# A four-layer transformer on one core: row weights loaded during the last attention, output done tile by tile, last handover re-ordered

## The reference

```
out = layer_norm(x + sigmoid(x @ gate_w + gate_b) * broadcast) * gamma + beta
```

## Time and profile before

| what | value |
|---|---|
| median of 3 runs | 4440.16 us (4436.63 to 4440.83) |
| profiled execution, its own time | 4444.07 us |
| its span, first to last instruction | 4442.3 us |
| mean granted PE clock | 0.928 of full speed |
| busy: PE, DVE, ACT, POOL | 85%, 55%, 36%, 33% |
| DMA moved | 585.42 MB, mean 132 GB/s |

### The profile page before, as it was taken

One profiled execution on the slowest core, in us unless ns is written; L12 is line 12 of the kernel. 1 busy time (PEld: TensorE's weight loads), 2 busy tenths in 40 slices (PEclk: granted clock), 3 DMA queues, 4 the chain that ended last, 5 costly groups with the idle time before them and its releaser, 6 DMA issues.

```text
span 4442.3 us, 53426 instructions
## 1 busy us (share of the span) xinstructions
PE 3769.3 (85%) x19032; PEld 2729.7 (61%) x19032; DVE 2423.0 (55%) x4270; ACT 1582.0 (36%) x2683; POOL 1447.2 (33%) x1732
## 2 busy tenths in 40 slices
PE   6877999999999999999999999999999998774300
PEld 4755776677657776777667766776577756442100
DVE  5643565366545664556546653665456644542477
ACT  4422434433443435343534344334434352220000
POOL 2421541244124521353124412441245213020266
PEclk9989999999999999999999999999999999766655
DMA  6464532444325332443235324443253323013222
GB/s 234 154 236 188 186 137 89 157 142 139 128 86 199 128 143 77 174 160 137 86 144 176 140 88 157 143 139 128 86 199 129 133 77 119 15 58 116 71 95 80
DMA packets 176147, 585.42 MB, mean 132 GB/s; under 512 B 14752, under 2 KB 15008, under 8 KB 171280
## 3 DMA queue, kind: packets, MB, share of 16 engines
q1 hardware_dynamic: 167056, 565.24, 35.7%
q10 hardware_dynamic: 8832, 16.78, 1.0%
HBM read 494.39 MB, written 87.05 MB: 131 GB/s over the span
## 4 chain that ended last, share of the span: by engine, by line
PE 65%; DVE 14%; POOL 7%; ACT 6%; issue 5%; DMA 3%; SPq 0%; DVEq 0%; POOLq 0%; ACTq 0%
PE ps_P L1577 24%; PE ps_Y L1577 10%; PE ps_E L1577 5%; PE ps_O L1577 4%; PE ps_O L1768 4%; PE ps_E L1750 3%; PE ps_T L1577 3%; PE ps_T L1729 3%; POOL pT_lo L721 3%; DVE pf L1164 2%; PE ps_T L1733 2%; POOL rstd L829 2%; ACT probs L957 1%; ACT pT_hi L844 1%; DVE stats L1070 1%
## 5 line engine op out<-in xcount | busy, mean ns | idle before, releaser
L1577 PE MATMUL ps_P<-XnT_hi,w_ring 128*128 128x512 f32 x3328 | 1079.5, 406 | 66.1 <-DVE XnT_lo L1046 14.5
L1577 PEld LDWEIGHTS ps_P<-XnT_hi,w_ring 128*128 128x128 f32 x3328 | 608.5, 191 | 230.4 <-issue 72.2
L1577 PE MATMUL ps_P<-XnT_lo,w_ring 128*128 128x512 f32 x1664 | 659.3, 396 | 0.0
L1270 DVE TENSOR_REDUCE row_max<-ps_T 128x1 fp32r<-128x384 f32 (+3 forms) x768 | 425.6, 595 | 277.1 <-PE ps_T L1733 277.0
L957 ACT ACTIVATE probs<-ps_E 128x512 f32<-128x512 f32 (+2 forms) x768 | 362.2, 524 | 451.1 <-PE ps_E L1750 303.5
L721 POOL TENSOR_TENSOR pT_lo<-pf,pT_hi 128x512 fp32r<-128x512 f32 x320 | 410.6, 1291 | 301.0 <-ACT pT_hi L844 296.0
L739 POOL TENSOR_SCALAR_AFFINE_SELECT probs<-probs 128x512 f32<-128x512 f32 x256 | 162.5, 635 | 1037.8 <-ACT probs L957 1037.8
L786 POOL TENSOR_TENSOR hT_lo<-hf,hT_hi 128x512 fp32r<-128x512 f32 x128 | 164.8, 1287 | 638.5 <-ACT hT_hi L844 638.5
L1577 PEld LDWEIGHTS ps_P<-XnT_lo,w_ring 128*128 128x128 f32 x1664 | 317.5, 191 | 70.5
L1577 PE MATMUL ps_Y<-w_big,hT_hi 128*128 128x512 f32 x896 | 333.8, 419 | 24.9 <-DVE y_acc L1294 12.6
L712 POOL TENSOR_TENSOR sines<-swapped,sinT 128x512 f32<-128x512 f32 x160 | 213.8, 1336 | 377.8 <-ACT swapped L844 371.7
(11 more groups left out here) (259 smaller groups left out, 7135.5 us busy)
## 6 DMA issues: line engine op xcount, KB each, us to landing
w_ring<-split_dram SPq DMA_DIRECT2D x412, 512.0 KB, 3.4
w_big<-split_dram SPq DMA_DIRECT2D x63, 2048.0 KB, 7.7
dec<-decay SPq DMA_DIRECT2D x32, 1024.0 KB, 4.8
split_dram<-w_ring SPq DMA_DIRECT2D x58, 512.0 KB, 4.2
split_dram<-w_big SPq DMA_DIRECT2D x36, 512.0 KB, 4.4
wo1w<-split_dram SPq DMA_DIRECT2D x8, 2048.0 KB, 7.8
gatew<-split_dram SPq DMA_DIRECT2D x8, 2048.0 KB, 10.2
X<-x SPq DMA_DIRECT2D x8, 1024.0 KB, 10.5
```

The costliest lines, as they stand in the source:

```text
L1270: dve.reduce_max(row_max[:, g % 2, i_, m0:m0 + len(heads)], ps[TB[half]][:, 0:len(heads) * w].rearrange("p (n s) -> p n s", s=w), AX_X)\
L1577: last = pe.matmul(dst, stat[s_], mov[m_], start=first_ and k == 0, stop=last_ and k == n - 1)
```

## The change

1. Memory: `d1w` and `d2w` get the place of `w_big`, `XnT` and `w_ring`, which are dead in the last attention; `aggw`, `bcw`, `thought`, `rows`, `bias1` lie over the feed-forward's buffers; the seven constants, gamma and beta lie in `X` and `y_acc`.
2. Row weights: in round 8 SP issues 16 transfers right after the handover's stores (`row_weights`), and nine of 1 MB in slots 8, 11, ..., 32 (`row_feed`). Block 7's x3 and gate are no longer stored; its last row is copied from `xr` into `rows`.
3. Handover of round 8: SP issues the ring units first. Block 6's front goes to `XnT` and its gate weights to `w_big`; its four gate products are made in slots 1, 2, 6 and 8 (banks E0, E1), the bias additions a slot later, the sigmoids at slot 10. DVE and POOL do block 7's layer-2 statistics, norms and residuals tile by tile, mixed with block 6's front.
4. After the slots: block 7's four gate products stand behind the first four phases of the row chain, its sigmoids behind the tenth. The chain uses one PSUM bank (P1) for all.
5. Broadcast: instead of a store and eight loads, eight matmuls of a column of the identity with `rows`, into all eight PSUM banks.
6. Output: tile by tile. The first norm isn't made as such: mean times rstd of all 32 tiles (`pd_shift`) is made once on POOL from moments kept from the gate's front; ACT scales x3 by its rstd (`fin_first`, the first of the two activations below), DVE subtracts the shift and adds the gated row. The last norm is ACT's scaling (`fin_last`) and a DVE instruction that subtracts the shift and adds x3. DVE works on tiles k, k-1 and k-3 in one iteration. POOL has only 128x1 operations. Loads go through a ring of three blocks, SP issues loads and stores, and block 7 is taken from `xr` and `y1`.

```diff
+FIN_RING, FIN_SKEW = 3, 3
+LAST_GATE_AT = (1, 2, 6, 8)
+SIGMOID_AT = 9
+FEED_AT = {8 + 3 * m: m for m in range(9)}
# SP, round 8
-                    x2_store(c)
                     for k in range(UNITS_A, UNITS_A + UNITS_C):
                         unit(n, k)
+                    gate_weights(c - 1)
+                    x2_store(c)
+                    row_weights(c)
...
+                        if n == NB and s in FEED_AT:
+                            row_feed(FEED_AT[s])
+                        if s == SLOTS - 1 and c == NB - 1:
+                            sp.dma_start(rows[c:c + 1, :], xr[P - 1:P, NT - 1, :]).then_inc(last_row_in, 16)
...
# POOL, output
+            for k in range(NF + 1):
+                if k < NF:
+                    fin_rstds(k, 0, eps_ffn)
+                if k:
+                    n = 4 + (k - 1) % 4
+                    fin_rstds(k - 1, 1, eps)
+                    pool.wait_ge(*fin_rstd[1].need(k - 1))
+                    pool.tensor_tensor(var_eps[:, n:n + 1], moments[:, n, 0:1], rstd[:, n:n + 1], ALU.mult).then_inc(*fin_shift2.hit(k - 1))
# ACT, output
+                act.activation(fin_h[:, k % 4, :], fin_place(k)[0], ACT.Copy, scale=pd_rstd[:, k:k + 1]).then_inc(*fin_h_done.hit(k))
...
+                act.activation(z, z, ACT.Copy, scale=rstd[:, n:n + 1]).then_inc(*fin_w.hit(k))
...
+            for k in range(NF + 1):
+                if k + 3 < NF:
+                    fin_first(k + 3)
+                if k:
+                    fin_last(k - 1)
# DVE, output
+            for k in range(NF + FIN_SKEW):
+                new, mid, old = k, k - 1, k - FIN_SKEW
+                    dve.tensor_tensor(z, ps[BC_BANKS[b]][:, :], z, ALU.mult)
...
+                    dve.scalar_tensor_tensor(z, z, rstd[:, n:n + 1], bet, ALU.mult, ALU.add)
...
+                    dve.scalar_tensor_tensor(z, fin_h[:, new % 4, :], pd_shift[:, new:new + 1], z, ALU.subtract, ALU.add)
...
+                    dve.scalar_tensor_tensor(z, z, var_eps[:, n:n + 1], x3_, ALU.subtract, ALU.add)
...
+                    fin_measure(new, 0, fin_sum.need(new))
+                    fin_measure(mid, 1, fin_affine.need(mid))
+                    fin_aggregate(new, 0)
+                    fin_aggregate(mid, 1)
+                    dve.scalar_tensor_tensor(z, z, moments[:, n, 0:1], gam, ALU.subtract, ALU.mult)
...
# PE
+                    if n == NB and s in LAST_GATE_AT:
+                        t = LAST_GATE_AT.index(s)
+                        gate_product(d, t, EB[t % 2], XnT, WB)
...
-            for t in range(NT):
-                gate_product(NB - 1, t)
+            for m, phase in enumerate(PHASES):
+                row_phase(*phase)
+                if m < NT:
+                    gate_product(NB - 1, m, FB[m], YnT, gatew)
+            for b in range(NB):
+                pe.matmul(ps[BC_BANKS[b]][:, :], ident[0:R, b:b + 1].to_broadcast([R, P]), rows[:, :], start=True, stop=True)
```

More of the change, by code:

```diff
@@ L64 @@
 WO_AT = {2: 2, 5: 3}
+PHASES = [("pre", 0, "T"), ("pre", 0, "agg")]
+PHASES += [("step", g, k) for g in range(K_STEPS) for k in ("T", "d1", "tr", "d2", "sum")]
+PHASES += [("post", 0, "T"), ("post", 0, "bc")]
+FIN_RING, FIN_SKEW = 3, 3
 SLOTS = 12 * NQ
@@ new lines, in build @@
+        ROW_INS = 16 * 25
+        NF = NB * NT
+        fin_in = [count(f"fin_in{n}", NB // FIN_RING + 1, step=32) for n in range(FIN_RING)]
+        fin_sent = [count(f"fin_sent{n}", NB // FIN_RING + 1, NT, step=16) for n in range(FIN_RING + 1)]
+        fin_bc, fin_shift = count("fin_bc", NB), sem("s_fin_shift")
+        fin_h_done, fin_w = count("fin_h", NF), count("fin_w", NF)
+        fin_gated, fin_sum, fin_scaled, fin_affine, fin_out = (count("fin_" + k, NF) for k in ("gated", "sum", "scaled", "affine", "out"))
@@ new lines, in build, with fin_place, moments_of @@
+        fin_stats, fin_moments = ([count(f"fin_{k}{n}", NF) for n in range(2)] for k in ("stats", "moments"))
+        fin_rstd, fin_shift2 = [count(f"fin_rstd{n}", NF) for n in range(2)], count("fin_shift2", NF)
+        BC_BANKS = ("P0", "P1", "T0", "T1", "E0", "E1", "O", "Y0")
+        def fin_place(k):
+            b, t = divmod(k, NT)
+            return (xr[:, t, :], y1[:, t, :]) if b == NB - 1 else (fin_x[:, b % FIN_RING, t, :], fin_z[:, b % FIN_RING, t, :])
+        def moments_of(kind, b, t):
+            n = KINDS.index(kind) * NT + t
+            return pd_moments[:, b * NT + t, :] if kind == "pd" else moments[:, n, :]
@@ L478, in build, with rstd_of @@
+        def rstd_of(kind, b, t):
+            n = KINDS.index(kind) * NT + t
+            return pd_rstd[:, b * NT + t:b * NT + t + 1] if kind == "pd" else rstd[:, n:n + 1]
         block = ctx.enter_context(nc.Block())
@@ new lines, in _ @@
+            for b in range(FIN_RING):
+                fin_load(b)
+            for k in range(NF):
+                b, t = divmod(k, NT)
+                slot = b % FIN_RING if b < NB - 1 else FIN_RING
+                sp.wait_ge(*fin_out.need(k))
+                sp.dma_start(out[b, t * P:(t + 1) * P, :], fin_place(k)[1]).then_inc(*fin_sent[slot].hit(b // FIN_RING if slot < FIN_RING else 0, t))
+                if t == NT - 1 and b + FIN_RING < NB - 1:
+                    sp.wait_ge(*fin_sent[slot].need(b // FIN_RING, NT - 1))
+                    fin_load(b + FIN_RING)
@@ L685, in _ @@
+            for slot in range(FIN_RING):
+                sp.wait_ge(*fin_sent[slot].need((NB - 2 - slot) // FIN_RING, NT - 1))
+            sp.wait_ge(*fin_sent[FIN_RING].need(0, NT - 1))
         @block.gpsimd
@@ L752, in _ @@
                     rope(n, 0)
-                if c >= 0:
+                if c >= 0 and n < NB:
                     for t in range(NT):
@@ L757, in _ @@
                         residual("qb", resid_b, c, t, X[c % 2][:, t, :], y_acc[:, t, :])
+                elif c >= 0:
+                    for t in range(NT + 3):
+                        if t < NT:
+                            rstds("qb", c, t)
+                        if t >= 1 and t <= NT:
+                            residual("qb", resid_b, c, t - 1, X[c % 2][:, t - 1, :], y_acc[:, t - 1, :])
+                        if t >= 3:
+                            rstds("pc", c, t - 3)
+                    pool.wait_ge(*down.need(c, NQ - 1, NT - 1))
+                    pool.memset(rows[:, :], 0.0).then_inc(s_rows_clear, 1)
                 if n < NB:
@@ new lines, in row_phase, with fin_rstds @@
+            def row_phase(stage, g, what):
+                if stage == "pre" and what == "T":
+                    row_rstds("pre", 0, 0, eps)
+                    row_rstds("pre", 0, 1, eps_ffn)
+                elif stage == "step" and what == "T":
+                    row_rstds("step", g, 0, eps_ffn)
+            for phase in PHASES:
+                row_phase(*phase)
+            def fin_rstds(k, m, eps_):
+                n = m * 4 + k % 4
+                pool.wait_ge(*fin_moments[m].need(k))
+                pool.tensor_tensor(var_eps[:, n:n + 1], moments[:, n, 1:2], eps_[:, :], ALU.add).then_inc(*ln_var.hit())
+                pool.wait_ge(*ln_var.need())
+                pool.tensor_tensor(rstd[:, n:n + 1], var_eps[:, n:n + 1], minus_half[:, :], ALU.pow).then_inc(*fin_rstd[m].hit(k))
@@ new lines, in _ @@
+            for m, phase in enumerate(PHASES):
+                row_phase(*phase)
+                if m < NT:
+                    gate_product(NB - 1, m, FB[m], YnT, gatew)
+            pe.wait_ge(*row_at(row, "post", 0, 2))
+            for b in range(NB):
+                if BC_BANKS[b] in empties:
+                    pe.wait_ge(*empties[BC_BANKS[b]])
+                pe.matmul(ps[BC_BANKS[b]][:, :], ident[0:R, b:b + 1].to_broadcast([R, P]), rows[:, :], start=True, stop=True)\
+                    .then_inc(*fin_bc.hit(b))
```

488 lines of the change are left out of this document (256 added, 232 removed).

## The result

The kernel after takes **4261.87 us** (median of 4 runs, 4257.73 to 4273.22) against 4440.49 us for the kernel before beside it: ratio 0.9607, 95% interval 0.9595 to 0.9618. The forecast was 4286 us with a range from 4268: the direction was right and the gain too small, 154 us forecast and 179 us measured, 6 us outside the range.

A forecast was written before the change was run, and what follows sets the result against it. TensorE is full up to 3737 us; a 705 us tail with little overlap follows, its output (266.6 us) longest. Terms -5.5-48.1+12.0-8.4-104.1 = -154.1 us, put on the median 4440.16, gave 4286 us, range 4268 to 4316.

The forecast's parts named there:

- Handover: Last down product to block 7's first query/key/value product: weights issued first and gate products gone, -14 us.
- Block 6's gates: Four gate products moved into attention slots: +3 us in slots 1 and 2, +5 in 6 and 8, bias additions +0.5.
- Late attention: Last attention, to the end of the residual: 25 added transfers on queue SP cost 0 us.
- Start of the row chain: Residual to first row statistic: weights already there, the chain waits only for DVE's last subtraction, -48.1 us.
- Block 7's gates: Four gate products between the row steps, partly in PE's waits: +12.0 us, bounds 7.2 and 18.5.
- Broadcast: Row's round trip through memory replaced by a K=32 matmul into PSUM: -8.4 us, bounds -8.6 and -7.9.
- Output: Final output stage: 4.85 us a tile plus 7.3 us end, 162.5 against 266.6 us, -104.1 us.
- Rival 1: Output: rstd late because POOL waits out DVE instructions, every tile stalls 0.75 us, +24 us, 4310 us; chance 0.12.
- Rivals 2 to 4: Attention held up, 4310 us, chance 0.08; weights not early, 4317 us, 0.03; POOL starved in the output, 4451 us, 0.01.

The follow-up runs named there:

- three variants that read 49 us: Kernel after with nine row-weight loads behind the last attention slot (4283.05 us), one more POOL addition per output tile (4272.29 us), or output not interleaved (4305.87 us).
- again: Kernel after, unchanged, run for more executions and a second profile: 4262.14 us, ratio 0.9605.
- the kernel with the cut: Kernel after with block 7's four gate products in the row chain cut from 12 matmuls to 1 each: 4260.59 us, ratio 0.9597.

## Why the prediction was wrong, point by point

In the first profile the tail got 33.5 us shorter than the sum had it: 10.3 in the row chain with block 7's gates, 7.4 where block 6's gates went, 6.9 in the output, 5.6 in the attention and 3.3 in the handover.

- **Handover, -14 forecast, -17.3 measured: right in mechanism.** The working gave 15.5 and took 1.5 off for POOL stretching VectorE's norms. Two norms were stretched and VectorE's work came out 0.9 us longer than worked out, but the product followed the front by 1.7 us less.
- **Block 6's gates, +8 forecast with +0.5 for DVE, +1.1 measured.** Priced by themselves they cost 5.3 to 6.6 us, so the term was 1.4 to 2.7 us too high, 1.3 of it in slots 6 and 8, where I took the higher price for a clock of 0.68; in this profile the slots ran at 1.00 (3787.5 to 3806.5). The larger part is what I had no term for: the matmuls around them ran faster. The kernel before with constants in its attention shows it without any gate: 40.7 us at a clock of 0.92, where it took 43.0 at 0.74. In the three variants that read 49 us the same slots ran at 0.78, and there the term would have been +6.0.
- **Late attention, 0 forecast, -5.6 measured.** Mostly the same cause: with the constants both kernels take 160 to 161 us at 0.98 and 0.99 (163 us at 0.96 in the two kernels that fill the row chain too).
- **Start of the row chain, -48.1 forecast, -48.2 measured: right**, and for the stated reason (VectorE's last subtraction ends it).
- **Block 7's gates, +12.0 forecast, +1.7 (again: +5.0) measured: the step that failed most.** Their own price was near: some 9 us for eleven twelfths of them against the kernel with the cut, or 10 to 11 us if the shortening of the nine weight products (8.2 us; again 43.6 instead of 49.7, 6.1) is added to what the stage grew by. The step that failed is that I priced an added product only by its own duration and left the products behind it at the durations of the kernel before, which had been measured behind idle stretches. Against the kernel with the cut, the gate products gave back 4.8 us (again: 2.7) in these nine; the other 3.4 us have no cause shown.
- **Broadcast, -8.4 forecast, -8.3 measured: right.**
- **Output, -104.1 forecast, -111.0 measured.** The sum of start-to-start times, 4.66 us, was right to 0.01. The failing term is the 0.2 us a tile that I put on top for the tight rstd (5.8 us), and the end, 6.2 us instead of 7.3. Rival 1 had the right weak place. It stayed away by next to nothing: with the extra POOL operation, rstd was 0.26 us later and a tile 0.27 us longer.
- **Rivals 2 to 4** did not come: the attention takes 170 us with the weights on SP's queue as without them at the same clock, the first row statistic is 8.0 us behind the residual, and POOL is busy for half of the output.
- **The range.** Its low end, 4268, allowed "a little below for a clock above 0.68", and all terms' lower bounds weren't to fall together. Three terms fell even below their own bounds: handover with block 6's gates (-16.2 us, bound -9.4), block 7's gates (+1.7, bound 7.2) and the output (-111.0, bound -110.2). The attention had no term at all. Three of the five better terms hang on one thing, the clock, and not on independent accidents.
- **How much is luck.** With the stages as the variants read them (49.0, 170.3 and 122.2 us) the first profile would have been 11.5 us longer, about 4269 us and just inside the range, as one of the eight executions was (4273.22). So that the number fell outside depends in part on how the clock fell; the missing term for it was wrong either way, and a stage with that lower clock was still 7 us shorter than forecast in the row chain.

The rule cited ahead, the lock of the ports that VectorE and GpSimd share (the Trainium skill, "SBUF — State Buffer", section "SBUF: two separate sides"), is borne out in the output for the small side. A power of 0.55 us takes 0.87 us when it starts 0.30 us behind the start of a scalar_tensor_tensor and 1.03 us at 0.13 us behind it; with the added operation in front of it, the ordinary addition of 0.19 us takes 0.64 us at 0.17 us behind it. In all three POOL ends as if it had begun 0.61 to 0.62 us behind VectorE's start. An addition only 0.03 us behind that start isn't held (0.19 us in each turn looked at, 4148.92 above). VectorE's own instructions, 0.74 to 0.78 us, show next to nothing of it, and so the rule's price falls on POOL alone there; in the handover, beside POOL's 128x512 additions, two of VectorE's norms paid.

## What to carry to other kernels

When work is moved into a stretch where TensorE waits between its products, price three things: its own duration, what of it falls into waits, and what the clock does to the matmuls behind it; in the row chain the third gave back 3 to 5 of some 9 us. Price a stage by more than one profile, too: the same instructions read 44 and 49 us. Look for the clock first: in a stage bound by other engines with a granted clock near 0.7, matmuls of constants in the waits, into a free bank, gained 4 to 11 us in the attention and 8 us in the row chain. And for an output bound by one engine, add up start-to-start times of unbroken runs and trust the sum where the wait that could break it is shown to be covered; put the risk in the range, not in the forecast.

## What the hardware showed that I had not expected

The clock falls differently in executions of the same instructions: the three stages from the first q/k/v product to the output took 44.1 to 49.0, 166.9 to 170.3 and 119.0 to 122.3 us in four profiles (two of the kernel after, one each of the variants with the POOL operation and with the serial output), 11 us between the ends together, while no other engine was busy longer. The Trainium skill, "TensorE: Matmul & The Clock Gate", section "What's actually happening", says that the number of a kernel's slow matmuls differs from run to run and that the ramp penalty is under 1% of a typical kernel span. The runs agree with both as far as they go: the 15 to 20 us gained by constants are under 0.5%. A comparison of two variants by one profile each can be wrong by as much: the cut of block 6's gates looked like 2.8 us and costs 5.3 to 6.6.
